# First attention with all heads turned in one visit, products in odd steps only, three banks for first scores

## What is computed

```python
x = _layernorm(x + _L0_attn_ref(x, L0_attn_w_qkv, L0_attn_w_out, L0_attn_b_out), axis=-1)
x = _layernorm(x + _L0_ffn_ref(x, L0_ffn_W_fc, L0_ffn_ln_w, L0_ffn_ln_b, L0_ffn_W_proj), axis=-1)
x = _layernorm(x + _L1_attn_ref(x, L1_attn_ln_g, L1_attn_ln_b, L1_attn_W_kv, L1_attn_W_x, L1_attn_W_xa, L1_attn_W_out), axis=-1)
x = _layernorm(x + _L1_ffn_ref(x, L1_ffn_w_gate, L1_ffn_w_up, L1_ffn_w_down), axis=-1)
```

## Time and profile before

| | |
|---|---|
| median of 3 runs | 1597.54 us (1597.44 to 1599.07) |
| profiled execution, own time | 1594.59 us |
| its span | 1592.8 us |
| PE, DVE, ACT, POOL busy, share of the span | 95%, 78%, 67%, 58% |
| from 200 to 500 us (first attention): PE, DVE, ACT, POOL busy | 295.86, 257.99, 230.47, 149.08 us of 300 |
| from 604.5 to 695.5 us (first feed-forward): the same | 88.15, 79.98, 72.17, 55.76 us of 91 |
| granted TensorE clock in both | 1.00 |
| POOL's waits for the parts' writes, L730, 32 times | 108.0 us |

### The profile page before, as it was taken

The page is one execution under the profiler, slowest core; times in us unless marked ns, Lnnn a source line. Parts: engine busy times, 40 slices in busy tenths (PEclk is TensorE's granted clock), DMA queues, the critical chain, the costliest instruction groups (busy, mean ns, idle before and its releaser), DMA issues. The chain is left out here.

```text
span 1592.8 us, 55776 instructions
## 1 busy us (share of the span) xinstructions
PE 1515.7 (95%) x17772; PEld 1143.4 (72%) x17772; DVE 1242.2 (78%) x3420; ACT 1068.5 (67%) x2596; POOL 928.5 (58%) x1065
## 2 busy tenths in 40 slices
PE   4899999999999999988999999999999999998998
PEld 3344444444444378875888988889889898897997
DVE  5788888888888678876877878878788787874666
ACT  0477777777777877764767777777777777774332
POOL 4445454454545146666777877778777787762222
PEclk7799999999999999996999999999999999999999
DMA  7444444444444200012222222222222222200111
GB/s 190 132 117 130 119 132 123 130 124 126 126 129 126 59 28 30 30 54 83 79 69 86 74 81 80 66 86 75 80 80 66 86 75 80 75 33 24 64 64 51
DMA packets 175160, 137.73 MB, mean 86 GB/s; under 512 B 13868, under 2 KB 144056, under 8 KB 175096
## 3 DMA queue, kind: packets, MB, share of 16 engines
q1 hardware_dynamic: 174128, 136.30, 29.6%
q10 hardware_dynamic: 968, 0.60, 0.1%
HBM read 68.95 MB, written 54.79 MB: 78 GB/s over the span
## 5 line engine op out<-in xcount | busy, mean ns | idle before, releaser
L900 DVE TENSOR_REDUCE shifts<-bank 128x2 bf16<-128x512 f32 x1024 | 688.2, 689 | 160.4 <-PE bank L1050 154.9
L848 ACT ACTIVATE probs<-bank 128x512 f32<-128x512 f32 x1024 | 576.7, 593 | 115.6 <-PE bank L1036 108.0
L998 PE MATMUL bank<-values,probs 64*128 64x129 f32 x8192 | 580.0, 277 | 3.9 <-DVE o_even L868 0.7
L998 PEld LDWEIGHTS bank<-values,probs 64*128 64x128 f32 x8192 | 527.1, 188 | 31.0 <-issue 10.9
L1036 PE MATMUL bank<-stack 49*128 49x256 bf16 x2048 | 385.3, 274 | 11.7 <-DMA stack<-shift_rows 6.3
L1050 PE MATMUL bank<-stack 48*128 48x256 bf16 x2048 | 381.6, 277 | 14.0 <-DVE shifts L900 6.5
L655 POOL TENSOR_TENSOR values<-mix,v_in 128x1024 f32<-128x1024 f32 x128 | 302.2, 2362 | 0.0
L664 POOL TENSOR_TENSOR o_odd<-o_odd,scaled 128x256 f32<-128x256 f32 x224 | 163.6, 730 | 162.9 <-ACT scaled L771 162.7
L1036 PEld LDWEIGHTS bank<-stack 49*128 49x128 bf16 x2048 | 158.2, 95 | 136.8 <-issue 70.9
L771 ACT ACTIVATE scaled<-bank,recips 128x128 f32<-128x128 f32 x448 | 138.0, 358 | 88.2 <-DVE recips L894 88.2
L1050 PEld LDWEIGHTS bank<-stack 48*128 48x128 bf16 x2048 | 148.3, 95 | 36.2 <-DVE shifts L900 16.2
(11 more groups left out here) (169 smaller groups left out, 2200.4 us busy)
## 6 DMA issues: line engine op xcount, KB each, us to landing
stack<-score_parts SPq DMA_DIRECT2D x64, 512.0 KB, 3.9
stack<-score_parts SPq DMA_DIRECT2D x256, 96.0 KB
score_parts<-parts SPq DMA_DIRECT2D x256, 64.0 KB, 2.1
score_parts<-parts SPq DMA_DIRECT2D x128, 96.0 KB, 2.3
score_parts<-parts SPq DMA_DIRECT2D x64, 192.0 KB, 2.2
x_in_f<-x_all SPq DMA_DIRECT2D x64, 128.0 KB, 2.0
score_parts<-parts SPq DMA_DIRECT2D x64, 128.0 KB, 2.3
x_in<-in_L_attn_x SPq DMA_DIRECT2D x32, 128.0 KB, 3.7
```

What stands on the lines that cost most here:

```text
L848: act.activation(probs[:, s % RING, :, :].rearrange("p t n -> p (t n)"), s2[s % 2][:, :], ACT.Exp, scale=scale).then_inc(exp_done, 1)
L900: dve.tensor_reduce(shifts[:, :, hf, col], s1[s % 2][:, :].rearrange("p (t n) -> p t n", t=TILES), op=ALU.max, axis=AX.X, negate=True).the ...
L998: return pe.matmul(pv_bank(h)[:, q * (D + 1):(q + 1) * (D + 1)], probs[rows, h % RING, t, q * P:(q + 1) * P], values[b.odd][rows, t, h, :] ...
```

## The change

- The products run in odd slots only, half a group each (1 to 15); each even slot has at most one visit to small operations. Two groups, eight heads, share one bank: the second group of a pair is written 16 rows lower. So there is one `pv` bank, two copies by ACT and one burst of four transposes at slot 8 in place of two bursts.
- The bank that comes free is a third one for first scores.
- Slots of the small operations: q 4, k 6, heads 8, o transposed and first half of the maxima 10, values 12, output product 14. The banks of some change.
- The normalization moves from DVE to ACT (slots 5 and 6), in the form scale times y plus shift, for which POOL computes two more small operations; POOL makes the copy of x for the values (`x_v`, two buffers) in place of ACT; its norm factor comes ahead of the split.
- The parts of q and k get two buffers.
- The sum of squares in the feed-forward is two additions (512 and 256 columns) in place of one reduction of 1024, with the aggregates between them.
- Two more steps of the first attention stand ahead of its loop.

```diff
-        self.shifts0 = 11 if first else 9
-        self.v, self.v_ahead = (14, 1) if first else (13, 2)
-        self.q, self.q_ahead = (3, 3) if first else (1, 2)
-        self.k = 5 if first else None
-        self.heads = (8, 6) if first else ()
-        self.ot = 11 if first else 9
-        self.out = 13 if first else 11
-        self.norm, self.norm_lag = (2, 2) if first else (15, 1)
+        self.shifts0 = 10 if first else 9
+        self.v, self.v_ahead = (12, 1) if first else (13, 2)
+        self.xt, self.xt_ahead = (0, 3) if first else (13, 3)
+        self.q, self.q_ahead = (4, 3) if first else (1, 2)
+        self.k = 6 if first else None
+        self.heads = 8 if first else None
+        self.ot = 10 if first else 9
+        self.out = 14 if first else 11
+        self.norm, self.norm_lag = (5, 2) if first else (15, 1)
+        self.stats_lag, self.factor_lag = (1, 2) if first else (1, 1)
...
-    s1, s2 = b[0:2], b[2:4]
-    pv, m0, m1 = (b[4:6], b[6], b[7]) if first else (b[4:7], b[7], b[7])
+    s1, s2 = (b[0:3], b[3:5]) if first else (b[0:2], b[2:4])
+    pv, m0, m1 = (b[5:6], b[6], b[7]) if first else (b[4:7], b[7], b[7])
+    s1_order = (0, 1, 2) * 4 + (0, 1) * 2 if first else (0, 1) * 8
...
+        def keep_x_for_v(i):
+
+            b = i.plus(2)
+            pool.wait_ge(xt_ready, times(i, 2, n))
+            wait(pool, v_in_psum, times(i, 0, n))
+            pool.tensor_tensor(x_v[b.odd][:, :], x_t[b.odd][:, :], core.zeros[:, :], op=ALU.add).then_inc(x_v_ready, 1)
 
         def step0(i, on):
+            if on(2):
+                keep_x_for_v(i)
             if on(-1):
                 add_bias(i)
+            if on(-2):
+                norm_factor(i)
             if on(slots.split):
                 split(i.plus(slots.split))
-            if on(-1):
-                norm_factor(i)
...
-            wait(pool, parts_written, times(b, -1, n) * (16 * writes))
-            pool.tensor_tensor(parts[:, 0, :, :], exact[:, :, :], zeros, op=ALU.add).then_inc(part0_ready, 1)
+            wait(pool, parts_written, times(b, -2, n) * (16 * writes))
+            pool.tensor_tensor(parts[b.odd][:, 0, :, :], exact[:, :, :], zeros, op=ALU.add).then_inc(part0_ready, 1)
...
-                if s == 3 and first and on(-1):
-                    take_heads(i.plus(-1), 3)
+                if s == 4 and first and on(-1):
+                    take_heads(i.plus(-1), 1)
+                if first and s in (slots.norm, slots.norm + 1) and on(-2):
+                    norm(i.plus(-2), (s - slots.norm,))
...
-                if s in (7, 11, 15) and first and on(0):
-                    take_heads(i, (s - 7) // 4)
+                if s == 12 and first and on(0):
+                    take_heads(i, 0)
...
-                if s == slots.xt and first and on(1):
-
-                    act.activation(x_v[:, :], x_t[i.plus(1).odd][:, :], ACT.Copy).then_inc(x_v_ready, 1)
-                if s == slots.xt and on(3):
+                if s == slots.xt + (1 if first else 0) and on(slots.xt_ahead):
...
+                if s == slots.heads and on(-1):
+                    recip_heads(i)
...
+                if s == slots.heads and on(-1):
+                    for sub in range(2):
+                        scale_heads(i, sub)
...
-                if first and s == slots.norm and on(-slots.norm_lag):
-                    b = i.plus(-slots.norm_lag)
-                    dve.wait_ge(rstd_ready, times(b, 0, n))
-                    dve.wait_ge(moments_ready, times(b, 0, n) * TILES)
-                    for t in range(TILES):
-                        dve.tensor_scalar(core.x_all[:, b.number(), t, :], y[:, t, :], moments[:, t, 0:1],
-                                          rstd[:, t:t + 1], ALU.subtract, ALU.mult).then_inc(x_ready, 1)
...
+            r, sub = g // 2, g % 2
...
+                if sub == 0:
+                    wait(pe, pv_taken, b.number() * regions + r)
             for a in range(4):
                 h = 4 * g + a
+                start = h * VW - sub * (VW // 2)
+                last = pe.matmul(pv[0][VW * a:VW * (a + 1), 0:TOK],
+                                 values[b.odd][:, t, :, :].rearrange("p h c -> p (h c)")[:, start:start + VW],
+                                 probs[:, h % RING, t, :], start=(sub == 0 and t == 0), stop=(sub == 1 and t == TILES - 1),
+                                 skip_group_check=True)
...
-                wait(pe, max_done, b.number() * HEADS + (s - 1))
+                wait(pe, max_done, s1_free(b, s))
...
             if s == slots.shifts1 and on(0):
 
-                pe.wait_ge(shift_rows_ready, i.number() * 2 + 1)
-                wait(pe, v_taken, times(i, 0, n))
+                wait(pe, xt_ready, times(i, 3, n))
                 shifts_turned(i, 1)
...
+            if s == slots.heads and on(-1):
+                b = i.plus(-1)
+                pe.wait_ge(pv_taken, times(i, -1, n) * regions)
+
+                wait(pe, qk_taken, times(i, 3, n) * 2 - 1)
+                wait(pe, y_ready, times(i, -2, n))
+                for t in range(TILES):
+                    for r in range(regions):
+                        last = pe.transpose(m1[:, (regions * t + r) * P:(regions * t + r + 1) * P],
+                                            heads_t[b.odd][:, r, t * P:(t + 1) * P], core.ident[:, :])
+                last.then_inc(heads_in_psum, 1)
...
+            if s == slots.ot and on(-1):
+                pe.wait_ge(o_ready, times(i, -1, n) * 2)
...
-                    if s in (1, 2) and on(-1):
-                        products_by_group(i.plus(-1), 3, s - 1)
-                    if s >= 5 and s % 4 in (1, 2) and on(0):
-                        products_by_group(i, (s - 5) // 4, s % 4 - 1)
+                    if s in (1, 3) and on(-1):
+                        products_by_group(i.plus(-1), 3, s // 2)
+                    if s >= 5 and s % 2 and on(0):
+                        products_by_group(i, (s - 5) // 4, (s - 5) % 4 // 2)
...
-                dve.tensor_reduce(square_sums[b.odd][:, :], squares[:, :, :].rearrange("p c n -> p n c"),
-                                  op=ALU.add, axis=AX.X).then_inc(sums_ready, 1)
+                wait_apart(dve, sums_ready, times(i, 0, n))
+                dve.tensor_tensor(half_sums[:, :, :], squares[:, 0:2, :], squares[:, 2:4, :], op=ALU.add).then_inc(halves_ready, 1)
...
+            if on(1):
+                b = i.plus(1)
+                dve.wait_ge(halves_ready, times(i, 1, n))
+                dve.tensor_tensor(square_sums[b.odd][:, :], half_sums[:, 0, :], half_sums[:, 1, :], op=ALU.add).then_inc(sums_ready, 1)
...
-    attn0.at(0, 1)
-    attn0.loop()
+    attn0.at(0, 1, 2, 3)
+    attn0.loop(4)
```

More of the change, by code:

```diff
@@ L469, in attention @@
     rest = sb("rest", [P, sides, TOK])
-    parts = sb("parts", [P, 3, sides, TOK], BF16)
+    parts = [sb(f"parts{k}", [P, 3, sides, TOK], BF16) for k in range(2)]
     shifts = sb("shifts", [P, TILES, 2, half_heads if first else P], BF16)
@@ L538, in attention, with s1_bank, s1_free @@
     rstd_ready = sem("rstd_ready")
-    minus_mean_ready = None if first else sem("minus_mean_ready")
-    norm_shift_ready = None if first else sem("norm_shift_ready")
+    minus_mean_ready = sem("minus_mean_ready")
+    norm_shift_ready = sem("norm_shift_ready")
     x_ready = sem("x_ready")
+    def s1_bank(s):
+        return s1[s1_order[s]]
+    def s1_free(b, s):
+        ago = min(k for k in range(1, HEADS + 1) if s1_order[(s - k) % HEADS] == s1_order[s])
+        return b.number() * HEADS + (s - ago + 1)
     banked = [h for h in range(HEADS) if h != BESIDE]
@@ L570, in parts_out @@
                 k = K_PART[s]
-                src = parts[:, k:k + 1, sides - 1, :]
+                src = parts[b.odd][:, k:k + 1, sides - 1, :]
                 if m > 1:
@@ L723, in split @@
                 wait(pool, part1_ready, times(b, -1, n))
-                pool.tensor_tensor(rest[:, :, :], exact[:, :, :], parts[:, 0, :, :], op=ALU.subtract).then_inc(rest_ready, 1)
+                pool.tensor_tensor(rest[:, :, :], exact[:, :, :], parts[b.odd][:, 0, :, :], op=ALU.subtract).then_inc(rest_ready, 1)
                 return
@@ L741, in last_part @@
                 pool.wait_ge(part1_ready, times(b, 0, n))
-            pool.tensor_tensor(parts[:, 2, :, :], rest[:, :, :], parts[:, 1, :, :], op=ALU.subtract).then_inc(parts_ready, 1)
+            pool.tensor_tensor(parts[b.odd][:, 2, :, :], rest[:, :, :], parts[b.odd][:, 1, :, :], op=ALU.subtract).then_inc(parts_ready, 1)
         return step0 if first else step1
@@ L972, in shifts_turned @@
                 to = SHIFTS_AT + t * P
-                last = pe.transpose(m0[:, :].bitcast(BF16)[0:half_heads if first else P, to:to + P], shifts[:, t, hf, :],
+                last = pe.transpose((m1, m0)[hf][:, :].bitcast(BF16)[0:half_heads if first else P, to:to + P], shifts[:, t, hf, :],
                                     core.ident_bf[:, :])
@@ L1128, in others_of_first @@
```

(13 more changed lines are left out.)

173 lines of the change are left out of this document (75 added, 98 removed).

## The result

The changed kernel takes 1578.16 us (median of 4 runs, 1576.97 to 1579.99), the kernel before, timed again beside it, 1597.49 (1593.65 to 1599.07). The ratio is 0.9887, with a 95% interval of 0.9868 to 0.9907: 19 us faster, where 15 were forecast. The prediction gives two ranges, 1576 to 1588 as its own and then 1566 to 1594; the time lies in both. The profiled execution took 1577.22, its span is 1574.7, 18.1 shorter than before.

What follows compares the result with a forecast made beforehand. PE's work and SP's stack-load path together were taken to bound the first attention, the loop through DVE's reduction the feed-forward: 1597.54 - 7 (attention) - 8 (feed-forward) = 1582.5 us, own range 1576 to 1588, wider range 1566 to 1594.

Steps and rivals of the forecast that it cites:

- The feed-forward: Two additions replace DVE's reduction: period from 4.54 to 4.2 us in 24 steps, -8 us (-6 to -10).
- Rival C: Feed-forward: DVE's addition is held by POOL's in each step, +3 us there, 1593.5 us in all; chance 0.08.
- The heads: Heads visit in the first attention: two bursts of four transposes become one, -0.58 us of PE per step.
- the joined scores: First attention: eight pairs of scores joined in place of four, each joining saving 0.11 us: -0.4 us per step.
- the products of slot 15: They now stand between the last score and the next step: from half load to PE's start 0.82 us, before 0.25.
- Wait (a) for o: PE waits for DVE's scalings ahead of the transposes of o at slot 10: 0.7 to 0.75 us, taken as 0.74.
- (b): Turned shifts at slot 2 wait for ACT's copy, which now stands after the first exponential: 0.35 us.
- (d): Near the step's start, the next score waits about 0.08 us for the exponential of slot 1.
- (c): y's addition goes ahead of maximum 15, which slot 1's first score needs: about 0.45 us after PE's start at the earliest.
- The step: Length of a first-attention step: 15.37 us in place of 15.63, in about 27 of 32 batches, -7 us.
- L = (W + path - g) / 2: First-attention step length from PE's work, SP's 16.3 us path and g, second half load's issue to PE's next start.
- W: PE's own work in a first-attention step: 15.2 us before, 14.1 without new waits, 15.27 with them.

Runs made afterwards that it cites:

- e1: The kernel before with the feed-forward's edit alone (two additions in place of the reduction): 1587.1 us, ratio 0.9951.
- e10: The changed kernel with two DRAM buffers for the parts and one row half's writes ahead of the shift rows: 1569.7 us, one execution.
- e2: The kernel before with two DRAM buffers for the parts of q and k: 1597.0 us, ratio 0.9992.
- e5: The changed kernel with o transposed at slot 12 and the maxima's first half turned at slot 10 in bank m0: 1571.8 us, ratio 0.9839.
- e6: e5 with two DRAM buffers for the parts and one row half written ahead of the shift rows: 1556.0 us, ratio 0.9741.
- e8: The changed kernel with two of its three first-score banks in turn, as before the change: 1590.1 us, ratio 0.9948.
- e9: The changed kernel with the feed-forward's reduction of before: 1589.6 us, ratio 0.9962.
- e3: The changed kernel with the heads' visit at slot 6 and k's product at slot 8: 1574.4 us, ratio 0.9871.
- e11: The changed kernel with POOL's addition to x in the feed-forward behind its wait for h_var: 1582.8 us, one execution.

## Why the prediction was right, point by point

- **The feed-forward** held in mechanism and size: -8 forecast, -8.9 measured, since PE's period is 4.15 and not 4.2. e1 shows it alone. The DVE piece took 1.48, 1.4 forecast.
- **Rival C** had a real mechanism. DVE's two additions and POOL's don't run side by side, as the Trainium skill (SBUF — State Buffer, Who interferes with whom) says: POOL's is held for some 0.5, DVE's second for 0.4. It cost nothing here for two reasons: from its seventh time on DVE's first addition started 0.01 to 0.11 ahead, so its own 0.67 wasn't prolonged (the fifth and the sixth, where POOL's was some 0.3 ahead, took 0.99 and 1.02); and the loop with it in it is still shorter than PE's 4.15.
- **The heads, the joined scores, the products of slot 15** held: the burst at slot 8 takes 0.59, scores of two steps 0.54, the time from the half load to PE's start of the next step went from 0.25 to 0.78 (0.82 forecast).
- **Wait (a) for o**: 0.74 forecast, 0.79 measured in each step, from DVE's queue counted instruction by instruction. The reciprocal takes 0.35 and not 0.25. **(b) to (d)**: PE's start of the step costs 0.52 beyond its work; 0.45 was forecast, with another share. 0.44 is the wait of slot 1's first score for DVE's maximum of slot 15, (c), and it stands in every step; the stack's 0.14 is hidden in it. ACT's copy, (b), was forecast at 0.35 and lengthens PE's block by 0.08 on average, and only in steps where the stack is late (e10: 0.00). The weight loads do stand idle for the copy, 0.37 in each step by the list above, but most of that lies beside the products. The second score of slot 3 waits 0.14, forecast 0.08.
- **The step**: 15.37 forecast, 15.38 measured. That agreement is better than the reasoning behind it, and in part luck. L = (W + path - g) / 2 fits every trace, since W is what is left of L when s is taken off. What failed is to take W as fixed when s changes. Without the stack's wait of 0.43, W rose from 15.20 to 15.53 in e2, as DVE's maximum of slot 15 then held PE for 0.39, and shortening the path gave 0.1 and not 0.43. I had read from the trace that PE waited for the stack in each step, and not asked what it would have waited for next. By the prediction W rises by 0.07 and the whole gain of 0.26 comes from the gap g. The runs show PE's chain in order, with its waits for DVE and ACT, as the bound, 15.53 before (e2) and 15.31 after (e10), and the path adds 0.1 and 0.07 to it. Where the path does bound, W hardly moves: 14.75 in e5, 14.79 in e6, and the formula with e5's own path and gap gives (14.75 + 15.54) / 2 = 15.14, as measured. That is a balance of measured terms and no test.
- **The third bank was mis-sized**: 0.1 of PE's work forecast, 0.29 per step measured by e8 (15.67 against 15.38). The waits of the kernel before, on which I sized it, are those of an order in which the rotations and scalings stand at other slots. In the new order two banks would be waited for 33.9 us from 200 to 500 us. So PE's chain went from 15.53 to 15.31 as the sum of -1.0 (heads and joinings) and +0.78 of waits: 0.59 in e2's step, 0.39 of it for the maximum of slot 15; 1.37 in e10's, 0.79 for o, 0.44 for the maximum of slot 15 and 0.14 at slot 3. The third bank only kept more from coming.
- **The filling** gained 2.9 us and the last two steps 2.1, where I had counted 27 steps at 0.26 in all and nothing at the ends. Draining lost 0.7. Together -9.0 for the attention, -7 forecast. Of this the filling's and the draining's parts are no larger than what kernels with the same attention differ by (198.7 and 201.5 us in the filling); e9, with the attention's part alone, gives -7.
- **Hidden edits**: no wait shows for the normalization on ACT, for POOL's copy of x or for its norm factor on anyone's path. What each is worth by itself wasn't tried.

## What to carry to other kernels

Before counting a wait's removal as a gain, look for the wait that stands behind it on the same in-order queue: the next semaphore in that queue whose update came later than the point to which the work would move up. A wait that the trace names in every step can be worth a quarter of its length (0.43 named, 0.10 won in e2), and shortening the same path is worth more once PE's chain is shorter (0.36 in e6). Look at when each semaphore's instruction ended, and not only at which engine the profile names: in e2 it names ACT, and DVE ended last. When small operations are put closer together on one engine, count the other engine's queue from the first of them to the one that is waited for; this gave 0.74 for 0.79 without a run, and e3 shows what it costs to leave out a reader of the shared bank.

## What the runs showed of the hardware

- A DVE addition with both inputs in SBUF and a POOL operation that reads SBUF hold each other: 782 ns in place of 393 and 1204 in place of 738 on average, as the two pairs of lines of e11 show. The one that starts first isn't prolonged: with POOL's 0.03 ahead, DVE's took 1.26 us and POOL's 0.74 (e1), with DVE's 0.01 ahead, they took 0.67 and 1.26. The reduction of before, with one input, ran beside the same POOL operation in every step, at 1.93, and POOL's took 0.73. The Trainium skill (SBUF — State Buffer, Who interferes with whom) says so, and these runs agree.
- PE's granted clock in the draining of the first attention differed between profiled executions with the same instructions there, and the stretch was some 10 us longer where it was lower. The windows view of e1 and of the kernel before, from the last half load to the feed-forward's sixth batch (the third last number is the granted clock):

```profile
532.50:601.00 68.50, 62.34 (x464) 38.41 (x465) 35.42 (x114) 46.41 (x101) 16.79 (x30) 0.83 0.09 28
```

```profile
529.50:589.50 60.00, 53.71 (x464) 35.24 (x464) 38.88 (x105) 45.74 (x102) 16.10 (x29) 1.00 0.10 33
```

In e1 a part of this stretch ran at the lower of the clock's two levels, 1.2 in place of 2.4 GHz, and the stretch is 8.5 us longer with the same 464 matmul records; in e2 it took 70.0 us at 0.80. Times of one kernel lay up to 17 us apart in these groups, which is why the verdicts here rest on steps read from the traces and on the medians of several runs.
